# Post-norm transformer layer on one core: a chunk's norm is finished in the third attention step of the next chunk and turned in the fourth, and its first step holds five half groups and nothing else

## The chip, the cores and the metric

The kernel runs on one core of a Trainium2 chip. The metric is device time in microseconds (us), the median of several runs; less is better. The engines are TensorE (matmuls and transposes, PE in the profile; its weight loads are listed as PEld), ScalarE (ACT), VectorE (DVE), GpSimd (POOL) and SyncE (SP), which issues most DMA transfers.

## What is computed

One layer on 2048 tokens of width 256, all float32: attention with 16 heads of 16 channels, a residual add and a layer norm, then a gated feed-forward network with int8 weights and scales, a residual add and a second layer norm.

```python
Q, K, V = X @ Wq + bq, X @ Wk + bk, X @ Wv + bv
scores = einsum('bhqd,bhkd->bhqk', q, k) / sqrt(16)
attn = softmax(scores, axis=-1)
out = einsum('bhqk,bhkd->bhqd', attn, v)          # channels come out as d, h
x = layernorm(X + out @ Wo + bo)
gate, up = silu((x @ w_gate) * s_gate), (x @ w_up) * s_up
x = layernorm(x + ((gate * up) @ w_down) * s_down)
```

## The kernel before

The queries are split into `CH` = 4 chunks of 512 tokens (0 to 3, `LAST` = 3) and the heads into `QUADS` = 4 groups of four. A **step** `s` (0 to 15) is one chunk with one group of heads; steps 4c to 4c+3 are chunk c's attention. A step has 16 **units**, one for each tile of 128 keys (`kt`). A unit's scores for four heads are two **groups** `g` of two heads, each of two banks of PSUM, in a ring of three groups; the matmuls run in fp32r. ScalarE takes the exponential of a group in one instruction (128x1024, line 654). In a **half group** it takes only the second bank; VectorE computes the exponential of the first bank's 512 columns by a polynomial on the bits, eight instructions in a row (lines 884 to 908), the first of which reads PSUM (`bits<-ps`). `poly_tiles(s)` says in which units a step has half groups. TensorE multiplies the probabilities with V two units later (`prob_times_v(u - 2)`, line 1254; `poly` is multiplied in an order in which its tile comes some units later) and sums a whole step in bank 6. At the step's end VectorE copies that bank out (`save_attn`, line 820), which happens while TensorE is in unit 1 of the next step; the next step's first product waits for the copy, and the copy for the last product. Every engine works its own program in order; semaphores tie them, and TensorE's score of group g waits until group g-3 has been read by ScalarE and, if that is a half group, by VectorE.

What is left for chunk c after its attention is spread by hand over the four steps of chunk c+1, which are its **stages** 0 to 3 (`stage = s % QUADS`, with `c = s // QUADS - 1` the finished chunk):

- stage 0: nothing of chunk c but the DMAs that move the results through DRAM into `at32`;
- stage 1: VectorE divides by the denominators (`scale_attn`), TensorE projects quarters 0 and 1 (`project_out`, four matmuls each, line 1276) behind units 8 and 15;
- stage 2: TensorE projects quarters 2 and 3, VectorE adds the first half to x (`ln1_add`, line 836);
- stage 3: the second add, statistics, variance (GpSimd raises it to the power -1/2) and scaling (lines 844 to 864);
- stage 0 of the chunk after: TensorE **turns** the normed tokens, four transposes for each half of the channels (`turn_y`, line 1294), behind units 3 and 8, and VectorE splits each half into a high and a low **part** (`ln1_parts`, lines 871 and 873) that the feed-forward matmuls read.

Chunk 2 has no such stage 0 in the attention: its turn and its parts stand in the feed-forward part, behind chunk 0's gate and up matmuls, where chunk 3's remaining work is spread as well. The attention's small matmuls of all chunks but the last use bank 7 (`FFN_BANK`), one after the other.

In the feed-forward part TensorE computes gate and up (line 1363) tile by tile, then down (line 1340), chunk by chunk. Two of its int8 weights are cast to fp32r by GpSimd (`wg`, `wu`, lines 576 and 577), into the place of the first group's keys, when the last score of step 12 has been computed:

```python
pool.wait_ge(scores_ready, 2 * UPS * (STEPS - QUADS + 1))
nc.gpsimd.tensor_copy(wg[:], gate8[:].bitcast(i8)).then_inc(ffn_w_ready, 1)
nc.gpsimd.tensor_copy(wu[:], up8[:].bitcast(i8)).then_inc(ffn_w_ready, 1)
```

Of the kernel before, what the change touches and what calls it, by code (L numbers as in the profile page):

```python
# [7 lines left out]
def layer_program(nc, X, Wq, bq, Wk, bk, Wv, bv, Wo, bo, w_gate, w_up, w_down, s_gate, s_up, s_down, out):  # L8
# [17 lines left out]
    MT = INTER // P  # L26
    HPB = P // HD
    NQ = 4
    QUADS = NH // NQ
# [26 lines left out]
    with ExitStack() as ctx:  # L56
# [179 lines left out]
        gate_up_free = sem("gate_up_free")  # L236
# [29 lines left out]
        FFN_BANK = 7  # L266


        LAST = CH - 1
# [6 lines left out]

        def turn_bank(c, ko):

            return FFN_BANK if c < LAST - 1 else 2 * ko

        QK = [(c, k) for c in range(CH) for k in (0, 2, 1, 3)]
        NQK = len(QK)
# [23 lines left out]

        def poly_tiles(s):

            return [6, 10, 13] if s == 0 else [2, 6, 10, 13] if s == 1 else [2, 5, 8, 11, 14] if s in (2, 3, 4) else [2, 6, 10, 13]


        def value_order(s):
# [385 lines left out]
        def _(dve):  # L698
# [124 lines left out]
            def scale_attn(c):  # L823

                dve.wait_ge(at_moved, 16 * KO * (c + 1))
                nc.vector.reciprocal(den[:], at32[:, :, HD, :]).then_inc(den_ready, 1)
                dve.wait_ge(den_ready, c + 1)
                nc.vector.tensor_tensor(at32[:, :, 0:HD, :], at32[:, :, 0:HD, :],
                                        den[:].unsqueeze(2).to_broadcast([P, KO, HD, UW]), ALU.mult
                                        ).then_inc(attn_scaled, 1)  # L830

            def ln1_add(c, b):

                bank = out_bank(c, b)
                dve.wait_ge(wo_psum, 2 * c + b + 1)
                nc.vector.tensor_tensor(x_by[:, 2 * b:2 * b + 2, c, :], x_by[:, 2 * b:2 * b + 2, c, :],
                                        ps[:, bank, :].rearrange("p (a b) -> p a b", a=2), ALU.add
                                        ).then_inc(ln1_sum, 1)
# [28 lines left out]
            def ln1_parts(c, ko):  # L867

                bank = turn_bank(c, ko)
                dve.wait_ge(yt_psum, KO * c + ko + 1)  # L870
                nc.vector.tensor_copy(qy[:, c, ko, 0, :], ps[:, bank, :]).then_inc(yt_hi_ready, 1)
                dve.wait_ge(yt_hi_ready, KO * c + ko + 1)
                nc.vector.tensor_tensor(qy[:, c, ko, 1, :], ps[:, bank, :], qy[:, c, ko, 0, :].bitcast(f32), ALU.subtract
                                        ).then_inc(yt_ready, 1)
# [37 lines left out]
            for s in range(STEPS):  # L912
                c = s // QUADS - 1
                if s:
                    save_attn(s - 1)
                tiles = [POLY_NO[2 * (UPS * s + kt)] for kt in poly_tiles(s)]


                stage = s % QUADS
                if s < 2:  # L920
                    for n in tiles:
                        exponentials(n)
                    continue
                exponentials(tiles[0])
                if c >= 0 and stage == 1:
                    scale_attn(c)
                if c >= 0 and stage == 2:
                    ln1_add(c, 0)
                if c >= 0 and stage == 3:
                    ln1_add(c, 1)  # L930
                if c >= 1 and stage == 0:
                    ln1_parts(c - 1, 0)
                exponentials(tiles[1])
                if c >= 0 and stage == 3:
                    ln1_stats(c)
                if c >= 1 and stage == 0:
                    ln1_parts(c - 1, 1)
                exponentials(tiles[2])
                if c >= 0 and stage == 3:
                    ln1_variance(c)  # L940
                for n in tiles[3:]:
                    exponentials(n)
                if c >= 0 and stage == 3:
                    ln1_scale(c)
            save_attn(STEPS - 1)

# [43 lines left out]
            for c in range(CH):  # L990
                for m in range(MT):
                    u = c * MT + m
                    if c and m == 0:
                        scale_down(c - 1)
                    if c == 1 and m == 0:
                        ln1_add(LAST, 0)
                        ln1_add(LAST, 1)
                    dve.wait_ge(silu_done, u + 1)
                    if u >= 2:

                        dve.wait_ge(h_ready, u - 1)
                    nc.vector.scalar_tensor_tensor(h32[:, u % 2, :], ps[:, 2 + u % 2, :], sup_c[:, m:m + 1],  # L1002
                                                   sg[:, u % 2, :], ALU.mult, ALU.mult).then_inc(gate_up_free, 1)
                    if m:
                        h_low(u - 1)
                    if m == MT - 1:
                        h_low(u)

                    if c and m in (2, 3):
                        ln2_stats(c - 1, m - 2)  # L1010
                    if c and m == 4:
                        ln2_variance(c - 1)
                    if c and m in (5, 6):
                        ln2_scale(c - 1, m - 5)


                if c == 0:
                    ln1_parts(LAST - 1, 0)
                    ln1_parts(LAST - 1, 1)
                    scale_attn(LAST)  # L1020
                if c == 1:
                    ln1_stats(LAST)
                    ln1_variance(LAST)
                    ln1_scale(LAST)
                if c == 2:
                    ln1_parts(LAST, 0)
                    ln1_parts(LAST, 1)
# [35 lines left out]
        def _(pe):  # L1063
# [35 lines left out]
            for n, (c, k) in enumerate(QK):  # L1099
# [11 lines left out]
                i, m = k // 2, k % 2  # L1111
# [170 lines left out]
            def turn_y(c, ko):  # L1282

                bank = turn_bank(c, ko)
                if ko == 0 and c >= LAST - 1:

                    pe.wait_ge(gate_up_free, MT - 1 if c < LAST else 3 * MT - 1)
                if ko == 0:
                    pe.wait_ge(ln1_ready, TPC * (c + 1))
                elif c < LAST - 1:  # L1290

                    pe.wait_ge(yt_ready, KO * c + 1)
                for j in range(TPC):
                    last = nc.tensor.transpose(ps[:, bank, j * P:(j + 1) * P], x_by[:, j, c, ko * P:(ko + 1) * P],  # L1294
                                               ident[:])
                last.then_inc(yt_psum, 1)
# [3 lines left out]
            for u in range(UNITS):  # L1300
                scores(2 * u)
                if u == 0:
                    project_v(V_LATE)
                scores(2 * u + 1)
                if u == 1:
                    project_v(V_LATE + 1)
                if u >= 2:
                    prob_times_v(u - 2)
                s, kt = u // UPS, u % UPS
                c, stage = s // QUADS - 1, s % QUADS  # L1310
                if c >= 0 and stage in (1, 2) and kt in (8, 15):
                    project_out(c, 2 * (stage - 1) + kt // 15)
                if c >= 1 and stage == 0 and kt in (3, 8):
                    turn_y(c - 1, kt // 8)
            prob_times_v(UNITS - 2)
            prob_times_v(UNITS - 1)

# [26 lines left out]
            for u in range(CH * MT):  # L1344
                c, m = u // MT, u % MT
                if u == MT:
                    for j in range(TPC):
                        project_out(LAST, j)
                if u == MT + 1:

                    pe.wait_ge(ln1_sum, 2 * CH)
                if m == 0 and c:

                    pe.wait_ge(yt_ready, KO * (CH if c == LAST else LAST))
                if m == 0 and c < LAST:
                    pe.wait_ge(yt_ready, KO * (c + 1))
                if u >= 2:

                    pe.wait_ge(gate_up_free, u - 1)
                for w, bank in ((wg, u % 2), (wu, 2 + u % 2)):  # L1360
                    for ko in range(KO):
                        for part in range(2):
                            last = nc.tensor.matmul(ps[:, bank, :], w[:, ko, m * P:(m + 1) * P], qy[:, c, ko, part, :],  # L1363
                                                    start=(ko == 0 and part == 0), stop=(ko == KO - 1 and part == 1))
                last.then_inc(gate_up_psum, 1)
                if m == MT - 1 and c in (0, LAST - 1):
                    turn_y(LAST if c else LAST - 1, 0)
                    turn_y(LAST if c else LAST - 1, 1)
                if m == MT - 1 and c < LAST:
                    for b in range(c * MT, (c + 1) * MT):  # L1370
                        down(b)
# [38 lines left out]
```

## Time and profile before

| what | value |
|---|---|
| median of 3 runs (lowest to highest) | 600.42 us (600.18 to 600.59) |
| profiled execution, its own time | 600.33 us |
| its span in the profile | 598.6 us |
| TensorE matmuls busy | 588.2 us, 98% |
| ScalarE busy | 506.6 us, 85% |
| VectorE busy | 442.4 us, 74% |
| GpSimd busy | 54.4 us, 9% |
| attention, first save to last | 76.3 to 495.8 us |

Busy time is the time in which at least one instruction of the engine is in flight. Matmuls overlap each other, so a busy TensorE says little about how much more it could do; an engine that waits shows in the waits, not in the busy share. The granted TensorE clock was 0.997 of full speed over the span.

### The profile page before, as it was taken

The numbers are of one execution on the slowest core, as the hardware profiler recorded it, in microseconds if no ns is written. First come the engines' busy times: TensorE is split into PE (matmuls) and PEld (weight loads), VectorE is DVE, ScalarE is ACT, GpSimd is POOL, SyncE is SP. The second block draws the span as 40 slices with busy tenths as digits, with TensorE's granted clock in tenths as the row PEclk, the third lists the DMA queues.
The fourth block names the chain that finished last, engine by engine and source line by source line (L and its number), as shares of the span: only waits on it lengthen the run. The fifth ranks groups of instructions, "written<-read, shape, count | busy, mean of one in ns | idle before, by whom it ended". The sixth has DMA issues, their size and how long they took to land.

```text
span 598.6 us, 10544 instructions
## 1 busy us (share of the span) xinstructions
PE 588.2 (98%) x3952; PEld 249.7 (42%) x3952; DVE 442.4 (74%) x812; ACT 506.6 (85%) x614; POOL 54.4 (9%) x51
## 2 busy tenths in 40 slices
PE   8999999999999999999999999999999999999995
PEld 7884222222222223223232322222323227988974
DVE  6673766989888767687676668888767696776876
ACT  4539999999999999999999999999999995253352
POOL 6606000000000000000000000003000001102021
PEclk9999999999999999999999999999999999999998
DMA  9466938112303020111211010112010000101102
GB/s 207 72 105 85 122 62 105 26 29 35 85 11 70 8 34 8 31 16 25 61 17 27 11 29 11 30 34 44 8 33 7 7 4 9 39 1 35 36 2 71
DMA packets 36185, 24.71 MB, mean 41 GB/s; under 512 B 24930, under 2 KB 30946, under 8 KB 35538
## 3 DMA queue, kind: packets, MB, share of 16 engines
q1 hardware_dynamic: 34740, 23.29, 23.1%
q10 hardware_dynamic: 1392, 0.72, 0.5%
q8 instruction: 32, 0.52, 0.4%
q14 instruction: 21, 0.17, 0.1%
HBM read 6.56 MB, written 4.33 MB: 18 GB/s over the span
## 4 chain that ended last, share of the span: by engine, by line
PE 96%; DVE 2%; ACT 1%; issue 0%; DMA 0%; SPq 0%; POOL 0%; POOLq 0%; ACTq 0%
PE ps L1254 42%; PE ps L1226 29%; PE ps L1363 10%; PE ps L1096 6%; PE ps L1340 4%; PE ps L1276 3%; PE ps L1067 1%; DVE attn_q L820 1%; PE ps L1294 1%; PE ps L1082 1%; ACT probs L654 0%; DMA out<-out_tmp 0%; SPq L511 0%; DVE xt_lo L722 0%; PE ps L1128 0%
## 5 line engine op out<-in xcount | busy, mean ns | idle before, releaser
L654 ACT ACTIVATE probs<-ps 128x1024 f32<-128x1024 f32 (+1 forms) x512 | 444.1, 1098 | 14.8 <-PE ps L1226 14.4
L1254 PE MATMUL ps<-probs,v_all 128*17 128x512 f32 x1916 | 269.0, 598 | 1.2 <-DVE attn_q L820 0.5
L1226 PE MATMUL ps<-q_slot,k_stack 51*128 51x512 f32 x1024 | 198.0, 458 | 0.0
L1226 PEld LDWEIGHTS ps<-q_slot,k_stack 51*128 51x128 f32 x1024 | 85.0, 184 | 220.1 <-ACT probs L654 206.1
L884 DVE TENSOR_SCALAR bits<-ps 128x512 int32<-128x512 f32 x66 | 45.5, 689 | 50.2 <-PE ps L1226 41.3
L1254 PE MATMUL ps<-poly,v_all 128*17 128x512 f32 x132 | 68.2, 599 | 0.0
L673 ACT ACTIVATE sg<-ps,sgate_c 128x512 f32<-128x512 f32 x32 | 22.0, 689 | 49.5 <-PE ps L1363 49.5
L1254 PEld LDWEIGHTS ps<-probs,v_all 128*17 128x17 f32 x1916 | 33.5, 95 | 61.2 <-issue 50.6
L908 DVE SCALAR_TENSOR_TENSOR poly<-poly,bits 128x512 f32<-128x512 f32 x66 | 47.2, 715 | 7.2 <-DVE poly L904 0.5
L904 DVE SCALAR_TENSOR_TENSOR poly<-poly,mant 128x512 f32<-128x512 f32 x66 | 45.7, 692 | 2.3
L895 DVE SCALAR_TENSOR_TENSOR poly<-mant 128x512 f32<-128x512 f32 x66 | 45.2, 684 | 0.0
L900 DVE SCALAR_TENSOR_TENSOR poly<-poly 128x512 f32<-128x512 f32 x66 | 45.1, 684 | 0.0
L820 DVE COPY attn_q<-ps 128x512 f32<-128x512 f32 x16 | 11.1, 691 | 45.3 <-PE ps L1254 45.3
L567 POOL TENSOR_TENSOR rstd<-var_eps,minus_half 128x4 f32<-128x4 f32 x4 | 4.1, 1028 | 402.1 <-DVE var_eps L856 402.1
L1002 DVE SCALAR_TENSOR_TENSOR h<-ps,sup_c,sg 128x512 f32<-128x512 f32 x32 | 23.9, 746 | 16.3 <-ACT sg L673 16.3
L1363 PE MATMUL ps<-qy,wg 128*128 128x512 f32 x128 | 35.6, 400 | 0.0
L1363 PE MATMUL ps<-qy,wu 128*128 128x512 f32 x128 | 34.4, 391 | 0.0
L1340 PE MATMUL ps<-wd,h_hi 128*128 128x256 f32 x128 | 31.1, 285 | 0.0
L1340 PE MATMUL ps<-wd,h_lo 128*128 128x256 f32 x128 | 30.9, 283 | 0.0
L890 DVE TENSOR_SCALAR bits<-bits 128x512 int32<-128x512 int32 x66 | 28.2, 427 | 2.3
L898 DVE TENSOR_SCALAR mant<-mant 128x512 f32<-128x512 f32 x66 | 28.2, 427 | 2.3
L887 DVE TENSOR_SCALAR mant<-bits 128x512 int32<-128x512 int32 x66 | 28.2, 427 | 2.3
(99 smaller groups left out, 452.9 us busy)
## 6 DMA issues: line engine op xcount, KB each, us to landing
q_slot<-qy SPq DMA_DIRECT2D x64, 64.0 KB
k_stack<-k_part SPq DMA_DIRECT2D x12, 256.0 KB
at_dram<-attn_q SPq DMA_DIRECT2D x64, 34.0 KB
at<-at_dram SPq DMA_DIRECT2D x8, 272.0 KB, 3.0
q_slot<-qy SPq DMA_DIRECT2D x64, 32.0 KB
x_tok<-in_L_attn_X SPq DMA_DIRECT2D x14, 128.0 KB, 5.9
k_stack<-k_part SPq DMA_DIRECT2D x12, 128.0 KB
out<-out_tmp SPq DMA_DIRECT2D x12, 128.0 KB, 2.2
```

Source lines behind the costliest of these rows:

```text
L654: nc.scalar.activation(probs[:, slot_of(g), first:2, :].rearrange("p a b -> p (a b)"), ps[:, 2 * ring + first:2 * ring + 2, :].rearrange(" ...
L884: nc.vector.tensor_scalar(bits[:], ps[:, 2 * ring, :], TO_BITS, LOWEST, ALU.mult, ALU.max).then_inc(poly_read, 1)
L887: nc.vector.tensor_scalar(mant[:], bits[:], FRACTION, ONE, ALU.bitwise_and, ALU.bitwise_or).then_inc(poly_bits, 1)
L895: nc.vector.scalar_tensor_tensor(res, mant_f[:], POLY["a"], mant_f[:], ALU.add, ALU.mult).then_inc(poly_square, 1)
L900: nc.vector.scalar_tensor_tensor(res, res, POLY["b"], res, ALU.add, ALU.mult).then_inc(poly_square, 1)
L904: nc.vector.scalar_tensor_tensor(res, res, POLY["c"], mant_f[:], ALU.add, ALU.mult).then_inc(poly_cube, 1)
L908: nc.vector.scalar_tensor_tensor(res, res, POLY["d"], bits_f[:], ALU.add, ALU.mult).then_inc(poly_done, 1)
L1096: last = nc.tensor.matmul(dst, w(ko), x(ko), start=(n == 0), stop=(n == len(terms) - 1))
L1226: last = nc.tensor.matmul(ps[:, 2 * ring + half, :], k_stack[s % QUADS][base:base + ROWS, p, kt * P:(kt + 1) * P], q_slot[slot][base:base ...
L1254: last = nc.tensor.matmul(ps[32 * hh:32 * hh + VW, ACC, :], v_all[:, tiles[hh], NQ * (s % QUADS) + hh, :], prob, start=(kt == 0), stop=(kt ...
L1340: last = nc.tensor.matmul(ps[:, 4 + i, 0:HID], h[:, m, i * P:(i + 1) * P], wd[:, m, :], start=(m == 0 and j == 0), stop=(m == MT - 1 and j ...
L1363: last = nc.tensor.matmul(ps[:, bank, :], w[:, ko, m * P:(m + 1) * P], qy[:, c, ko, part, :], start=(ko == 0 and part == 0), stop=(ko == K ...
```

## The change

The half groups: step 8 and step 12 get five instead of four. The turn of chunks 0 to 2 comes in stage 3, at the same units 3 and 8; chunk 2's leaves the feed-forward part. What made the norm ends in stage 2. For that the projections stand behind units 8 and 13 of stage 1, and 3 and 7 of stage 2. Chunk 3's work stays.

```diff
         def turn_bank(c, ko):
 
-            return FFN_BANK if c < LAST - 1 else 2 * ko
+            return FFN_BANK if c < LAST else 2 * ko
...
-            return [6, 10, 13] if s == 0 else [2, 6, 10, 13] if s == 1 else [2, 5, 8, 11, 14] if s in (2, 3, 4) else [2, 6, 10, 13]
+            return ([6, 10, 13] if s == 0 else [2, 6, 10, 13] if s == 1 or s > QUADS and s % QUADS else
+                    [2, 5, 8, 11, 14])
...
+                if c >= 0 and stage == 2:
+                    ln1_add(c, 0)
                 exponentials(tiles[0])
                 if c >= 0 and stage == 1:
                     scale_attn(c)
+                if c >= 0 and stage == 3:
+                    ln1_parts(c, 0)
+                exponentials(tiles[1])
                 if c >= 0 and stage == 2:
-                    ln1_add(c, 0)
+                    ln1_add(c, 1)
+                    ln1_stats(c)
                 if c >= 0 and stage == 3:
-                    ln1_add(c, 1)
-                if c >= 1 and stage == 0:
-                    ln1_parts(c - 1, 0)
-                exponentials(tiles[1])
-                if c >= 0 and stage == 3:
-                    ln1_stats(c)
-                if c >= 1 and stage == 0:
-                    ln1_parts(c - 1, 1)
+                    ln1_parts(c, 1)
                 exponentials(tiles[2])
-                if c >= 0 and stage == 3:
+                if c >= 0 and stage == 2:
                     ln1_variance(c)
                 for n in tiles[3:]:
                     exponentials(n)
-                if c >= 0 and stage == 3:
+                if c >= 0 and stage == 2:
                     ln1_scale(c)
...
                 if c == 0:
-                    ln1_parts(LAST - 1, 0)
-                    ln1_parts(LAST - 1, 1)
                     scale_attn(LAST)
...
-                if c >= 0 and stage in (1, 2) and kt in (8, 15):
-                    project_out(c, 2 * (stage - 1) + kt // 15)
-                if c >= 1 and stage == 0 and kt in (3, 8):
-                    turn_y(c - 1, kt // 8)
+                if c >= 0 and stage == 1 and kt in (8, 13):
+                    project_out(c, kt // 13)
+                if c >= 0 and stage == 2 and kt in (3, 7):
+                    project_out(c, 2 + kt // 7)
+                if c >= 0 and stage == 3 and kt in (3, 8):
+                    turn_y(c, kt // 8)
...
-                if m == MT - 1 and c in (0, LAST - 1):
-                    turn_y(LAST if c else LAST - 1, 0)
-                    turn_y(LAST if c else LAST - 1, 1)
+                if m == MT - 1 and c == LAST - 1:
+                    turn_y(LAST, 0)
+                    turn_y(LAST, 1)
```

What this does to the order of instructions is best seen at three places. First VectorE at the start of stage 2 of chunk 0 (step 6); before, the rows are the save of step 5, the eight instructions of the first half group's polynomial, and the first add to x:

```order
L820 COPY attn_q_110<-ps 128x512
L884 TENSOR_SCALAR bits<-ps 128x512
L887 TENSOR_SCALAR mant<-bits 128x512
L890 TENSOR_SCALAR bits<-bits 128x512
L895 SCALAR_TENSOR_TENSOR poly<-mant 128x512
L898 TENSOR_SCALAR mant<-mant 128x512
L900 SCALAR_TENSOR_TENSOR poly<-poly 128x512
L904 SCALAR_TENSOR_TENSOR poly<-poly,mant 128x512
L908 SCALAR_TENSOR_TENSOR poly<-poly,bits 128x512
L836 TENSOR_TENSOR x_tok<-x_tok,ps 128x2x256
```

The same place after (line numbers are one higher):

```order
L821 COPY attn_q_110<-ps 128x512
L837 TENSOR_TENSOR x_tok<-x_tok,ps 128x2x256
L885 TENSOR_SCALAR bits<-ps 128x512
L888 TENSOR_SCALAR mant<-bits 128x512
L891 TENSOR_SCALAR bits<-bits 128x512
L896 SCALAR_TENSOR_TENSOR poly<-mant 128x512
L899 TENSOR_SCALAR mant<-mant 128x512
L901 SCALAR_TENSOR_TENSOR poly<-poly 128x512
```

The add has moved ahead of the polynomial, between the save and the reading of the half group's scores.

Second, TensorE in units 13 to 15 of stage 1 and unit 0 of stage 2 (the scores are `q_slot,k_stack`, the products with V `probs,v_all` and `poly,v_all`, a quarter of the projection `wo,at`). Before:

```order
L1226 MATMUL ps<-q_slot_104,k_stack_93 128x512 x4
L1254 MATMUL ps<-probs,v_all 17x512 x4
L1226 MATMUL ps<-q_slot_104,k_stack_93 128x512 x4
L1254 MATMUL ps<-poly,v_all 17x512
L1254 MATMUL ps<-probs,v_all 17x512 x3
L1226 MATMUL ps<-q_slot_104,k_stack_93 128x512 x4
L1254 MATMUL ps<-probs,v_all 17x512 x4
L1276 MATMUL ps<-wo,at_108 128x256 x2
L1226 MATMUL ps<-q_slot_103,k_stack_94 128x512 x4
```

After:

```order
L1224 MATMUL ps<-q_slot_104,k_stack_93 128x512 x4
L1252 MATMUL ps<-probs,v_all 17x512 x4
L1274 MATMUL ps<-wo,at_108 128x256 x2
L1224 MATMUL ps<-q_slot_104,k_stack_93 128x512 x4
L1252 MATMUL ps<-poly,v_all 17x512
L1252 MATMUL ps<-probs,v_all 17x512 x3
L1224 MATMUL ps<-q_slot_104,k_stack_93 128x512 x4
L1252 MATMUL ps<-probs,v_all 17x512 x4
L1224 MATMUL ps<-q_slot_103,k_stack_94 128x512 x4
```

The quarter now stands behind unit 13, which has a half group, instead of behind unit 15.

Third, VectorE in the feed-forward part behind the last h of chunk 0. Before:

```order
L987 TENSOR_TENSOR h_lo<-h_105,h_hi 128x512 x2
L871 CAST qy<-ps 128x512
L873 TENSOR_TENSOR qy<-ps,qy 128x512
L871 CAST qy<-ps 128x512
L873 TENSOR_TENSOR qy<-ps,qy 128x512
L826 RECIPROCAL den<-at_108 128x64
L828 TENSOR_TENSOR at_108<-at_108,den 128x2x512
```

After:

```order
L987 TENSOR_TENSOR h_lo<-h_105,h_hi 128x512 x2
L827 RECIPROCAL den<-at_108 128x64
L829 TENSOR_TENSOR at_108<-at_108,den 128x2x512
L953 TENSOR_TENSOR r_tmp<-ps,sdown_b 128x512 x2
L837 TENSOR_TENSOR x_tok<-x_tok,ps 128x2x256 x2
```

The parts of chunk 2 are gone from there, and the scaling of chunk 3 follows h at once.

## Rows read from the trace of the kernel before

**Rows 1.** Page, part 1: busy us (share of the span) and instructions of each engine.
```profile
PE 588.2 (98%) x3952; PEld 249.7 (42%) x3952; DVE 442.4 (74%) x812; ACT 506.6 (85%) x614; POOL 54.4 (9%) x51
```

**Rows 2.** Waits: engine line waited for, us in total, times, longest us.
```profile
PEld ps L1226 <- ACT probs L654: 206.1, 288, 0.9
```

**Rows 3.** Timeline of TensorE, units 14 and 15 of step 9, unit 0 of 10.
```profile
319.90 0.73 PE L1226 MATMUL ps<-q_slot,k_stack 51*128 51x512 f32 x4
...
321.55 0.73 PE L1226 MATMUL ps<-q_slot,k_stack 51*128 51x512 f32 x4
...
324.26 0.73 PE L1226 MATMUL ps<-q_slot,k_stack 51*128 51x512 f32 x4
```

**Rows 4.** Timelines of ScalarE from four starts (merged rows: start, us, count).
```profile
319.15 5.21 ACT L654 ACTIVATE probs<-ps 128x512 f32<-128x512 f32 x6
...
319.62 4.74 ACT L654 ACTIVATE probs<-ps 128x1024 f32<-128x1024 f32 x5
...
320.53 3.83 ACT L654 ACTIVATE probs<-ps 128x1024 f32<-128x1024 f32 x4
324.80 1.94 ACT L654 ACTIVATE probs<-ps 128x1024 f32<-128x1024 f32 x2 [0.44 <-PE ps L1226]
```

**Rows 5.** Windows, save to save, steps 4 to 8, 15: us, then busy us by engine.
```profile
158.31:185.51 27.20, 27.20 (x194) 7.63 (x194) 23.37 (x41) 27.20 (x34) 0.00 (x0) 1.00 0.31 68
185.51:214.48 28.97, 28.97 (x202) 8.63 (x202) 20.52 (x36) 28.15 (x34) 0.00 (x0) 1.00 0.14 23
214.48:243.28 28.80, 28.67 (x202) 8.52 (x202) 19.41 (x35) 27.97 (x33) 0.00 (x0) 1.00 0.12 19
243.28:270.73 27.45, 27.31 (x194) 7.63 (x194) 22.40 (x47) 27.45 (x33) 1.06 (x1) 1.00 0.13 20
270.73:298.71 27.98, 27.98 (x202) 8.04 (x202) 21.50 (x37) 27.87 (x34) 0.00 (x0) 1.00 0.20 41
...
469.67:495.77 26.10, 25.66 (x185) 6.89 (x186) 22.40 (x47) 26.08 (x30) 1.02 (x1) 1.00 0.05 7
```

**Rows 6.** Timeline at units 2 and 3 of step 10: save, half group, scores.
```profile
327.69 0.69 DVE L820 COPY attn_q<-ps 128x512 f32<-128x512 f32 x1 [4.01 <-PE ps L1254]
328.29 0.68 DVE L884 TENSOR_SCALAR bits<-ps 128x512 int32<-128x512 f32 x1
...
329.41 0.73 PE L1226 MATMUL ps<-q_slot,k_stack 51*128 51x512 f32 x4
```

**Rows 7.** Timelines: end of step 4 (five half groups); end of step 12 with the casts.
```profile
179.13 0.69 DVE L884 TENSOR_SCALAR bits<-ps 128x512 int32<-128x512 f32 x1 [0.27 <-PE ps L1226]
...
180.31 0.73 PE L1226 MATMUL ps<-q_slot,k_stack 51*128 51x512 f32 x4
...
181.38 0.43 DVE L898 TENSOR_SCALAR mant<-mant 128x512 f32<-128x512 f32 x1
...
183.23 0.69 DVE L908 SCALAR_TENSOR_TENSOR poly<-poly,bits 128x512 f32<-128x512 f32 x1
...
184.39 0.61 PE L1254 MATMUL ps<-poly,v_all 128*17 128x512 f32 x1
...
407.22 0.69 DVE L904 SCALAR_TENSOR_TENSOR poly<-poly,mant 128x512 f32<-128x512 f32 x1
407.39 2.27 POOL L576 CAST wg<-gate 128x2048 fp32r<-128x2048 int8 x1 [30.41 <-PE ps L1226]
408.02 2.19 DVE L908 SCALAR_TENSOR_TENSOR poly<-poly,bits 128x512 f32<-128x512 f32 x1
409.62 2.34 POOL L577 CAST wu<-up 128x2048 fp32r<-128x2048 int8 x1
```

**Rows 8.** Chain that ended last, feed-forward part: start us, us, what.
```profile
510.77 0.87 PE ps L1294 x8
...
519.32 3.46 PE ps L1276 x16
```

**Rows 9.** Timeline of VectorE, scaling of chunk 3's results.
```profile
516.80 1.22 DVE L828 TENSOR_TENSOR at<-at,den 128x1024 f32<-128x1024 f32 x1
```

More of the change, by code:

```diff
@@ L1284, in turn_y @@
                 bank = turn_bank(c, ko)
-                if ko == 0 and c >= LAST - 1:
-                    pe.wait_ge(gate_up_free, MT - 1 if c < LAST else 3 * MT - 1)
+                if ko == 0 and c == LAST:
+                    pe.wait_ge(gate_up_free, LAST * MT - 1)
                 if ko == 0:
                     pe.wait_ge(ln1_ready, TPC * (c + 1))
-                elif c < LAST - 1:
+                elif c < LAST:
                     pe.wait_ge(yt_ready, KO * c + 1)
```

## Prediction

> **What bounds the kernel now.** I read the page first, then the waits, then windows from save to save, and last the timeline around the places where the change puts work. The page says TensorE is busy 98% and ScalarE 85% [rows 1]. The waits correct this: TensorE's loads of weights for the scores stood idle 206.1 us for ScalarE's exponentials, in 288 waits [rows 2]. So in the attention the two are nearly matched, and each step must be read for itself.
>
> TensorE needs 321.55 - 319.90 = 1.65 us for a unit (one key tile) when nothing holds it, 26.3 us for a step of 16. A quarter of an output projection put behind a unit adds 324.26 - 321.55 - 1.65 = 1.06 us [rows 3]. ScalarE starts a full exponential every 320.53 - 319.62 = 0.91 us, and a half one lasts 319.62 - 319.15 = 0.47 until the next [rows 4]: 32 x 0.905 - 4 x 0.43 = 27.2 us for a step with four half groups, 26.8 with five.
>
> The windows between saves agree [rows 5]. Plain steps: 27.20 with five half groups (step 4), 27.45 with four (step 7), ScalarE's limit. Steps 5 and 6 with two projections each: 28.97 and 28.80, TensorE's limit of 26.3 + 2 x 1.06 = 28.4 and some edges. Step 8 with two turns and four half groups: 27.98. Steps 9 to 14 repeat 5 to 8, 5 and 6 within 0.02; step 15 is 26.10, since no scores follow it. Behind the attention the chain is TensorE's alone [rows 8].
>
> **The change, part by part**, on the profiled execution's own 600.33 us (span 598.6 and 1.7 around it); the median of the runs shown is 600.42.
>
> (a) Steps 8 and 12 lose both turns and get a fifth half group, so they become like step 4: 27.98 - 27.20 = 0.78, twice, **-1.56**.
>
> (b) Steps 7, 11 and 15 get two turns at units 3 and 8, among the tiles (2, 6, 10, 13) that step 8 has now: 27.98 - 27.45 = 0.53, three times, **+1.59**. Step 15's turn, of chunk 2, is new in the attention.
>
> (c) The feed-forward part loses that turn: 0.87 us of the chain [rows 8], and the down products behind it need only h that is long there. Next would be the projection of chunk 3, which waits for VectorE's scaling of `at32`. It began at 519.32; scaling ended at 516.80 + 1.22 = 518.0, behind 2.8 us of parts that go away [rows 8, 9]. That covers it; without the cover the gain would go. Bounds 0 and 0.87, taken near the row: **-0.83**.
>
> (d) In stage 1 the second projection moves from unit 15 to 13, in stage 2 from 8 and 15 to 3 and 7. TensorE's work stays, and there TensorE is the limit. Only ScalarE's lag behind it grows. A waiting ScalarE starts 324.80 - 324.26 = 0.54 after a unit's first score. At unit 15 it lost 324.80 - (320.53 + 4 x 0.905) = 0.65. With 1.06 put in behind unit 13, where a half group has just used up the slack, the score of unit 14 moves from 319.90 to 320.96, its exponential from 320.53 to 321.50: 0.97 lost [rows 3, 4]. Units 3 and 7 also stand behind half groups. If all of that is paid, it is 0.3 in stage 1 and as much in stage 2; if TensorE's time alone counts, 0. I take +0.27 a chunk, near the middle, as TensorE is the limit in both steps but not in stage 3, where the lag is carried: **+0.8**, between 0 and 1.9.
>
> (e) VectorE's adds, statistics and scaling come one stage earlier. Stage 2 will hold what stage 3 holds now and one add of 0.7 more, 23.1 us of 28.8 [rows 5], and is covered. One place is tight: the first add now stands between the save and the half group of unit 2, so that group's reading of PSUM starts 328.29 - 327.69 = 0.60 later and ends at 329.57. The second score pair of unit 3 writes the same bank, 0.34 behind the first at 329.41, its weights 0.2 before that [rows 6]: late by 0.0 to 0.1, three times. I count 0.1, inside (d)'s figure. If the cover went, it would be 0.6 each.
>
> (f) The fifth half group of step 12. GpSimd casts the two FFN weights right behind the last score of step 12: 407.39 for 2.27 us, 409.62 for 2.34. VectorE's last multiply of tile 13's polynomial started at 408.02 and took 2.19 us, against 0.69 elsewhere: it ended at 410.21, 0.55 behind the first cast's end at 409.66. And the casts' own ends are 1.75 behind VectorE's releases: 407.22 + 0.69 = 407.91 to 409.66, 410.21 to 411.96 [rows 7]. The two engines exclude each other here, instruction by instruction. Today that falls on one multiply and nobody waits. The fifth half group's last tile is 14, a unit later. Take step 4, which has it: the read starts 179.13, the last score ends 180.31 + 0.73 = 181.04, the polynomial ends 183.23 + 0.69 = 183.92, and TensorE wants it at 184.39 [rows 7]. The slack is 0.47. The casts would start at 181.09 on that scale, with the last four operations (2.5 us, 181.38 to 183.92) still to come, the last three of them with two inputs in SBUF like the multiply that was held. The first cast holds them 1.7 us. The second starts with the first's end, finds a chain of separate operations and gets in between them, 1.75 more. The polynomial ends at 183.92 + 1.7 + 1.75 = 187.4, and TensorE's product comes 3.0 late. Behind it stand the save of step 12, the first products of step 13 and its fourth unit, and ScalarE is out of scores by then: nothing covers it. With one cast alone it is 1.7 - 0.47 = 1.2. Bounds: 0, if VectorE's operations slip through, and 3.0. By the row nearest (2.19 for 0.69, handed over at the cast's end) both casts count: **+2.9**.
>
> [...] If only what the row shows is held, two-input operations, the chain stops at 181.72 and not at 181.38, the product is 2.6 late, and the sum is 602.9.
>
> **Sum:** -1.56 + 1.59 - 0.83 + 0.8 + 2.9 = +2.9. 600.33 + 2.9 = 603.2; the median lies 0.1 above the profiled execution at most, so **603.2**.
>
> **Rivals.**
> - *The casts hold only one operation, or none*, because VectorE, once let in at 409.7, keeps the port to the end of its chain. One cast: 0.0 + 1.2, 601.5. None: 600.3. For it: today the waiting multiply did get in ahead of the second cast. Against it: three or four operations are left, not one, and the second cast starts right at the first's end. Chance 0.14 for one, 0.08 for none.
> - *ScalarE is the limit everywhere*, so each gap on it is lost for good. (d) is then its upper end, 1.9, and the sum 604.3. For it: it is busy 27.20 of 27.20 us in step 4; against it, 28.15 of 28.97 and 27.97 of 28.80 in steps 5 and 6, with TensorE at work throughout [rows 5]. It decides if the two projection steps grow together by over 0.4. Chance 0.10.
> - *The change pays, faster.* The turns of stage 3 cost nothing, because ScalarE enters the stage with scores in hand, and the chain of step 12 ends in time: -1.56 - 0.83 = -2.4, 597.9. It needs the polynomial to be done within 0.47 us of slack; from there on it decides. For it: in plain steps TensorE has 27.45 - 26.3 = 1.1 us over. Against it: step 8's 0.53 for the same turns, and (f). Chance 0.05.
> - *The sum as it stands*, both casts, (d) within its bounds: 0.63. Its own range is 602.2 to 604.2.
>
> **How the numbers follow.** The time is the last case's. The range leaves out the case of no cast and the fast one (0.13) and the far end of the ScalarE case: 600.9 to 604.6. About 0.2%, 1.2 us, is what a measurement of this kernel tells from no change: faster than 599.2 is the fast case, 0.06 with an edge; up to 601.6 the none case and most of the one-cast case, 0.18; the rest, 0.76, slower.
>
> **What the profile after would show.** Right: a last multiply (or an operation or two before it) of step 12's fifth polynomial that is stretched to about 2 us, TensorE waiting about 3 us for `poly` in unit 1 of step 13, and the save of step 12 about 3 later than now; step 8 at 27.2; steps 7 and 11 near 28; 0.8 less between the last save and chunk 3's projection. ScalarE's gaps largest behind unit 13 of stage 1 and units 3 and 7 of stage 2. Wrong: that save within 0.5 of where it is (then (f) fails), steps 9 and 10 together over 0.4 longer ((d) or (e) too low), a wait of TensorE for VectorE's add in bank 7, or a wait of chunk 3's projection for `at32`.

## The result and the profile after

The changed kernel takes **606.05 us** (median of 4 runs, 604.72 to 606.22), the kernel before 600.50 in the same job: a ratio of 1.0089, 95% interval 1.0076 to 1.0102. I forecast 603.2, between 600.9 and 604.6. The direction was right; the size was not, and the time lies outside the range. The profiled execution took 605.95 us with a span of 604.2, 5.6 more than before.

Part 1 of the page and the first wait of TensorE's loads hardly moved [rows 1, 2], but for VectorE's 11.3 us more (two more half groups and the time in which it is held), so the averages do not show where the 5.6 us are:

```profile
PE 591.5 (98%) x3952; PEld 250.7 (41%) x3952; DVE 453.7 (75%) x828; ACT 505.5 (84%) x614; POOL 53.9 (9%) x51
```

```profile
PEld ps L1224 <- ACT probs L655: 203.4, 292, 1.7
```

The windows from save to save come next, as in [rows 5], for steps 5 to 8, 12, 13 and 15.

```profile
core 0: us, PE busy (x) PEld busy (x) DVE busy (x) ACT busy (x) POOL busy (x), PEclk, DMA share, GB/s
184.98:214.06 29.08, 29.08 (x202) 8.73 (x202) 20.52 (x35) 27.89 (x33) 0.00 (x0) 1.00 0.13 21
214.06:243.20 29.14, 29.14 (x202) 8.81 (x202) 23.00 (x49) 27.84 (x34) 1.06 (x1) 1.00 0.12 19
243.20:271.18 27.98, 27.98 (x202) 8.03 (x202) 21.50 (x37) 27.86 (x34) 0.00 (x0) 1.00 0.14 22
271.18:298.38 27.20, 27.20 (x194) 7.65 (x194) 23.38 (x41) 27.20 (x34) 0.00 (x0) 1.00 0.20 42
384.55:415.54 30.99, 28.11 (x194) 7.68 (x194) 26.65 (x42) 28.34 (x34) 4.02 (x2) 0.95 0.21 43
415.54:445.97 30.43, 30.43 (x202) 8.88 (x202) 20.62 (x35) 26.95 (x31) 0.00 (x0) 0.93 0.10 15
475.08:501.71 26.63, 26.41 (x193) 7.29 (x194) 21.50 (x37) 26.50 (x31) 0.00 (x0) 1.00 0.05 7
```

Steps 5 to 8 are 29.08, 29.14, 27.98 and 27.20 long, against 28.97, 28.80, 27.45 and 27.98. So what is left of chunk 0 costs 0.20 more than before. Chunk 1 repeats it but for the last of its four steps: step 12 is 30.99 long where step 8 is 27.20, and step 13 is 30.43 where step 9 is 29.06. Of the windows shown, these two alone have a granted clock below 1.00.

The timeline at the end of step 12 shows GpSimd's casts and VectorE's fifth polynomial, as in [rows 7]; the number behind the start is the duration.

```profile
406.89 0.68 DVE L896 SCALAR_TENSOR_TENSOR poly<-mant 128x512 f32<-128x512 f32 x1
407.34 1.98 POOL L577 CAST wg<-gate 128x2048 fp32r<-128x2048 int8 x1 [57.47 <-PE ps L1224]
407.61 2.00 DVE L899 TENSOR_SCALAR mant<-mant 128x512 f32<-128x512 f32 x1
409.28 2.08 POOL L578 CAST wu<-up 128x2048 fp32r<-128x2048 int8 x1
409.53 2.38 DVE L901 SCALAR_TENSOR_TENSOR poly<-poly 128x512 f32<-128x512 f32 x1
411.94 0.69 DVE L905 SCALAR_TENSOR_TENSOR poly<-poly,mant 128x512 f32<-128x512 f32 x1
412.74 0.69 DVE L909 SCALAR_TENSOR_TENSOR poly<-poly,bits 128x512 f32<-128x512 f32 x1
```

Two operations are held, each until a cast ends: line 899, 0.43 us elsewhere, takes 2.00 and ends 0.29 behind the first cast; line 901, 0.69 elsewhere, takes 2.38 and ends 0.55 behind the second. The polynomial ends at 413.43. The same place on TensorE:

```profile
409.82 0.87 PE L1224 MATMUL ps<-q_slot,k_stack 51*128 51x512 f32 x4
413.57 1.01 PE L1252 MATMUL ps<-poly,v_all 128*17 128x512 f32 x1 [2.88 <-DVE poly L909]
415.41 1.22 PE L1224 MATMUL ps<-q_slot,k_stack 51*128 51x512 f32 x4
416.56 1.91 PE L1252 MATMUL ps<-probs,v_all 128*17 128x512 f32 x8
418.40 1.22 PE L1224 MATMUL ps<-q_slot,k_stack 51*128 51x512 f32 x4
419.55 1.05 PE L1252 MATMUL ps<-probs,v_all 128*17 128x512 f32 x8
```

TensorE waits 2.88 us for the polynomial. When it starts again, eight products take 1.91 us, and only from 419.55 on again 1.05. Windows around the place show the granted clock (first number behind the engines' columns):

```profile
407.50:410.50 3.00, 3.00 (x24) 0.87 (x16) 2.96 (x3) 3.00 (x4) 3.00 (x2) 1.00 0.33 54
410.70:412.70 2.00, 0.00 (x0) 0.00 (x0) 1.90 (x2) 2.00 (x3) 0.66 (x1) 1.00 0.44 75
412.72:419.55 6.83, 5.98 (x25) 1.34 (x25) 4.51 (x8) 2.00 (x4) 0.00 (x0) 0.50 0.09 16
419.60:424.00 4.40, 4.40 (x36) 1.12 (x36) 3.07 (x5) 4.40 (x6) 0.00 (x0) 1.00 0.11 15
```

TensorE idles from 410.69 on. At 412.72, still idle, its granted clock falls to 0.50, 1.2 GHz in place of 2.4, and it stays there for 6.83 us. ScalarE is busy 2.00 of these 6.83 us; the rest of the time it waits for scores. The windows of before stand at 1.00 [rows 5]. The Trainium skill ("TensorE: Matmul & The Clock Gate", Part 1: The HAM clock gate) says that an idle TensorE is throttled to 1.2 GHz and that renewed activity releases the throttle. The rows agree: 0.50 came in the idle stretch, and 1.00 came back at 419.55, with TensorE at work again since 413.57. I had not weighed it.

### The profile page after: what moved, and what is told of

The parts are those of the page before. It is cut to its first block, busy times and chain, and to the rows that moved or that the text cites. A ratio compares the mean times of both kernels' runs of the same rounds, so it can differ in the third digit from the quotient of the medians.

```text
span 604.2 us, 10569 instructions
## 1 busy us (share of the span) xinstructions
PE 591.5 (98%) x3952; PEld 250.7 (41%) x3952; DVE 453.7 (75%) x828; ACT 505.5 (84%) x614; POOL 53.9 (9%) x51
## 4 chain that ended last, share of the span: by engine, by line
PE 96%; DVE 2%; ACT 0%; issue 0%; DMA 0%; SPq 0%; POOL 0%; POOLq 0%; DVEq 0%; ACTq 0%
PE ps L1252 41%; PE ps L1224 30%; PE ps L1363 10%; PE ps L1094 6%; PE ps L1340 4%; PE ps L1274 3%; PE ps L1065 1%; PE ps L1292 1%; PE ps L1080 1%; DVE poly L901 0%; DVE mant L899 0%; DMA out<-out_tmp 0%; SPq L512 0%; DVE xt_lo L723 0%; ACT probs L655 0%
## 5 line engine op out<-in xcount | busy, mean ns | idle before, releaser
L885 DVE TENSOR_SCALAR bits<-ps 128x512 int32<-128x512 f32 x68 | 46.9, 690 | 46.2 <-PE ps L1224 37.6
L1252 PE MATMUL ps<-poly,v_all 128*17 128x512 f32 x136 | 71.1, 605 | 2.9 <-DVE poly L909 2.9
L905 DVE SCALAR_TENSOR_TENSOR poly<-poly,mant 128x512 f32<-128x512 f32 x68 | 47.1, 692 | 2.4
L901 DVE SCALAR_TENSOR_TENSOR poly<-poly 128x512 f32<-128x512 f32 x68 | 48.2, 709 | 0.0
L896 DVE SCALAR_TENSOR_TENSOR poly<-mant 128x512 f32<-128x512 f32 x68 | 46.6, 685 | 0.0
L899 DVE TENSOR_SCALAR mant<-mant 128x512 f32<-128x512 f32 x68 | 30.6, 450 | 2.4
```

What stands on the lines that cost most here:

```text
L885: nc.vector.tensor_scalar(bits[:], ps[:, 2 * ring, :], TO_BITS, LOWEST, ALU.mult, ALU.max).then_inc(poly_read, 1)
L896: nc.vector.scalar_tensor_tensor(res, mant_f[:], POLY["a"], mant_f[:], ALU.add, ALU.mult).then_inc(poly_square, 1)
L899: nc.vector.tensor_scalar(mant_f[:], mant_f[:], POLY["e"], POLY["scale"], ALU.add, ALU.mult).then_inc(poly_line, 1)
L901: nc.vector.scalar_tensor_tensor(res, res, POLY["b"], res, ALU.add, ALU.mult).then_inc(poly_square, 1)
L905: nc.vector.scalar_tensor_tensor(res, res, POLY["c"], mant_f[:], ALU.add, ALU.mult).then_inc(poly_cube, 1)
L1252: last = nc.tensor.matmul(ps[32 * hh:32 * hh + VW, ACC, :], v_all[:, tiles[hh], NQ * (s % QUADS) + hh, :], prob, start=(kt == 0), stop=(kt ...
```

## The experiments

Each ran on one chip beside the kernel before, which had a median of 600.54 (first four kernels), 600.36 (next four) and 600.14 us (last four). "Attention" below is the time from the first save to the last in the trace: 419.48 before, 425.96 with the change.

### What step 12 costs

**Four half groups in step 12.**

```
-[2, 6, 10, 13] if s == 1 or s > QUADS and s % QUADS else
+[2, 6, 10, 13] if s in (1, 12) or s > QUADS and s % QUADS else
```

> The changed kernel with step 12 back at four half groups (tiles 2, 6, 10, 13); all else as changed. Theory A (the casts hold the fifth polynomial, TensorE idles 2.9 us, its granted clock falls to 0.5 for 6.8 us and that costs 2.3 more): steps 12 and 13 lose the 5.2 us that they are too long, step 12 is 0.25 longer as a plain step with four half groups, so 606.05 - 5.15 + 0.25 = 601.2, and no stretch of 0.5 clock before the end. Rival B (only the stall of 2.9 comes from the casts, the rest of the miss lies in the moved projections and turns): 606.05 - 2.9 + 0.25 = 603.4.

Measured: 601.35 us, ratio 1.0016 (1.0006 to 1.0025), as theory A had it. Step 12 is 27.62 and step 13 29.09 long, and the granted clock is 1.00 until TensorE's last product is done. Rival B falls.

**Both casts later.**

```
+pool.wait_ge(poly_done, POLY_NO[2 * (UPS * 13 + 6)] + 1)
 nc.gpsimd.tensor_copy(wg[:], gate8[:].bitcast(i8)).then_inc(ffn_w_ready, 1)
+pool.wait_ge(poly_done, POLY_NO[2 * (UPS * 13 + 13)] + 1)
 nc.gpsimd.tensor_copy(wu[:], up8[:].bitcast(i8)).then_inc(ffn_w_ready, 1)
```

> The changed kernel with GpSimd's two casts of FFN weights put where VectorE is idle in step 13: the first behind the polynomial of tile 6 (idle 2.8 us there), the second behind that of tile 13 (idle 4.1 us). Theory A: the fifth half group of step 12 is then free, steps 12 and 13 are as 8 and 9, 606.05 - 5.15 = 600.9. Rival B: 603.2. Rival C (the fifth half group makes step 12 late by itself, since VectorE ends too late there whatever GpSimd does): step 12's stall stays, 606.

Measured: 600.17 us, ratio 0.9993 (0.9984 to 1.0002), 0.7 better than theory A said; behind the last product it has 0.8 less than the changed kernel (see the last section). Windows of steps 12 and 13:

```profile
384.77:411.97 27.20, 27.20 (x194) 7.63 (x194) 23.38 (x41) 27.20 (x34) 0.00 (x0) 1.00 0.21 43
411.97:441.04 29.07, 29.07 (x202) 8.73 (x202) 20.52 (x36) 27.88 (x33) 3.78 (x2) 1.00 0.13 21
```

Both casts now run in step 13, 1.89 us each, and nobody waits. Step 12 with five half groups is as long as step 8. The attention is 420.83, so the collision is worth 425.96 - 420.83 = 5.13 us, all of it in steps 12 and 13. Rivals B and C fall.

**One cast later.** The first added wait of the last edit is left out, the second stays.

> The changed kernel with only the second cast moved behind tile 13 of step 13; the first stays behind the last score of step 12. Theory A: the first cast holds one operation of the polynomial by 1.6 us, of which the slack covers 0.5: TensorE idles 1.2 us, and against the 600.2 of the kernel with both casts moved that gives 601.4 if so short an idle time leaves the granted clock at 1.0, or 603.7 if the clock falls here too. Rival C (one cast is enough for the whole stall): 606.

Measured: 601.71 us, ratio 1.0025 (1.0015 to 1.0035). The rows of VectorE, GpSimd and TensorE at the end of step 12:

```profile
407.83 1.98 POOL L577 CAST wg<-gate 128x2048 fp32r<-128x2048 int8 x1 [57.45 <-PE ps L1225]
408.10 1.99 DVE L900 TENSOR_SCALAR mant<-mant 128x512 f32<-128x512 f32 x1
410.01 0.68 DVE L902 SCALAR_TENSOR_TENSOR poly<-poly 128x512 f32<-128x512 f32 x1
412.36 0.59 PE L1253 MATMUL ps<-poly,v_all 128*17 128x512 f32 x1 [1.18 <-DVE poly L910]
```

One operation is held, TensorE waits 1.18 us (1.2 expected), and the granted clock stays at 1.00; the products behind take 0.6 as ever. The attention is 421.89, 1.06 above that of both casts moved. Rival C falls: the stall of 2.88 needs both casts.

**Work in the wait.** TensorE, in place of idling, transposes the identity 24 times into a bank that nobody reads.

```
+if u == UPS * 13 - 1:
+    pe.wait_ge(yt_ready, KO * 2)
+    for i in range(24):
+        nc.tensor.transpose(ps[:, FFN_BANK, 0:P], ident[:], ident[:])
 if pairs[0] in POLY_NO:
     pe.wait_ge(poly_done, POLY_NO[pairs[0]] + 1)
```

> The changed kernel with 24 transposes of the identity into bank 7, which nobody reads, put before TensorE's wait for the polynomial of tile 14 of step 12: 24 x 0.11 = 2.6 us of work that lies in the idle 2.88 us. Theory A: the polynomial comes as late as before, the save of step 12 stays at 415.5, but the granted clock stays at 1.0 and step 13 is about 2.3 us shorter: 606.05 - 2.3 = 603.7. Rival D (the clock falls for another reason, or its fall costs nothing since ScalarE is the limit): 606.0.

Measured: 603.70 us, ratio 1.0049 (1.0034 to 1.0065). TensorE's rows at the place:

```profile
411.15 2.84 PE L1246 MATMUL ps<-ident 128*128 128x128 f32 x24
414.02 0.60 PE L1256 MATMUL ps<-poly,v_all 128*17 128x512 f32 x1
415.88 1.05 PE L1256 MATMUL ps<-probs,v_all 128*17 128x512 f32 x8
```

The product comes as late as in the changed kernel (414.02 against 413.57, in a run whose first save came 0.53 later); the transposes end as the polynomial does (413.99 and 413.96), so they add next to nothing to the wait. The granted clock stays at 1.00, and the eight products further on take 1.05 and not 1.91. The attention is 423.51. So the 5.13 us split: 423.51 - 420.83 = 2.68 for the wait, 425.96 - 423.51 = **2.45 for the clock**. Rival D falls.

**The kernel before with a fifth half group in step 12**, its turns kept there: `[2, 5, 8, 11, 14] if s in (2, 3, 4, 12) else`.

> The kernel before with a fifth half group in step 12 alone (tiles 2, 5, 8, 11, 14), its turns kept there. Theory A: ScalarE has 0.4 less to do, but the casts hold the last polynomial and the clock falls: 600.4 - 0.4 + 2.9 + 2.3 = 605.2, or more, since VectorE has the parts of the turn in that step too. Rival B: 602.9, with the clock whole. Rival C (the collision needs the rest of the change): 600.0.

Measured: 608.84 us, ratio 1.0139 (1.0123 to 1.0154), 3.6 above theory A's figure; rivals B and C fall. The collision and the clock are there: TensorE waits 3.30 us for the polynomial, and its clock is at 0.5 from 414.58 for 6.83 us. Part of the rest is what theory A named only as "or more". (The profiled execution took 607.19, 1.65 below the median, so the trace does not show all of it.) The waits from 380 to 412 us have a line that the kernel before lacks:

```profile
PE ps L1226 <- DVE bits L884: 1.8, 1, 1.8
```

TensorE's scores wait 1.8 us because VectorE, with five polynomials and two turns' parts in one step (busy 29.13 us, its held time included), reads a score bank late. So the collision needs only the fifth half group, not the rest of the change. The other wait is absent where the turns are out of the step, as in the run with both casts moved.

### What the moved projections cost

**Stage 1's second projection back behind unit 15**, both casts moved: `kt in (8, 15)` in place of `(8, 13)`.

> Both casts moved, and stage 1's second projection back behind unit 15 (stage 2 keeps units 3 and 7). Placement costs ScalarE's lag: the gap behind unit 13 is 0.97 and behind unit 15 it was 0.65, so 0.3 a chunk, 600.2 - 0.9 = 599.3. Rival: TensorE is the limit in that step and the place of its work costs nothing, 600.2.

Measured: 599.83 us, ratio 0.9991 (0.9982 to 1.0000); the attention is 420.48, 0.35 shorter. I expected 0.9, the rival nothing; less than half of the 0.9 came. ScalarE's gap (from one exponential's start to the next, less the 0.91 of a full one) behind the projection did fall from 0.97 to 0.64, but that behind unit 3 of stage 2, now nearer, rose from 0.89 to 0.94 with 0.14 more at unit 2.

**Stage 2 at units 5 and 8**, the rest as in the last: `kt in (5, 8)` in place of `(3, 7)`.

> Both casts moved, stage 1's projections behind units 8 and 15 as before the change, and stage 2's behind 5 and 8 in place of 3 and 7. If it is the half group just ahead (units 2 and 6) that makes the places 3 and 7 dear, stages 1 and 2 come down from 58.12 towards the 57.7 of before: 599.8 - 3 x 0.3 = 598.9. If it is that the projections stand close together, or VectorE's statistics in stage 2: 599.8.

Measured: 599.35 us, ratio 0.9989 (0.9980 to 0.9998), the only version whose interval lies below 1, by a hair. Windows of steps 9 to 12:

```profile
298.51:327.47 28.96, 28.96 (x202) 8.63 (x202) 20.53 (x36) 28.16 (x34) 0.00 (x0) 1.00 0.14 22
327.47:356.47 29.00, 28.85 (x202) 8.60 (x202) 23.10 (x49) 27.81 (x33) 1.02 (x1) 1.00 0.12 19
356.47:384.45 27.98, 27.98 (x202) 8.05 (x202) 21.51 (x38) 27.86 (x34) 0.00 (x0) 1.00 0.11 17
384.45:411.65 27.20, 27.20 (x194) 7.64 (x194) 23.39 (x42) 27.20 (x34) 0.00 (x0) 1.00 0.22 45
```

Step 9 is back at the 28.98 of before, as it was in the last run already; step 10 is 0.2 longer than before. The attention is 420.09, another 0.39 shorter than in the last run, where I expected 0.9; 599.35 lies half-way between the two theories, so the run decides for neither. ScalarE's gaps in step 10 say where the rest sits: 0.64 and 0.73 behind units 5 and 8, against 0.62 and 0.67 behind 8 and 15 before the change, and 0.25 more behind unit 6, the half group that follows the first of them. Why that half group loses 0.25 is left open: the short distance of the two places and VectorE's work there were not told apart.

**Smaller pieces**, with both casts moved and in the kernel before: each projection as two stretches, each turn as two times two transposes. The added lines of the first of the two kernels, without those that let `project_out` and `turn_y` do half of their work; the kernel before has its own places:

```
+PIECES = {1: (8, 10, 12, 14), 2: (3, 5, 7, 8), 3: (3, 4, 7, 8)}
+if c >= 0 and stage and kt in PIECES[stage]:
+    i = PIECES[stage].index(kt)
+    if stage < 3:
+        project_out(c, 2 * (stage - 1) + i // 2, (i % 2,))
+    else:
+        turn_y(c, i // 2, (2 * (i % 2), 2 * (i % 2) + 1))
```

> Both casts moved, and TensorE's additions in pieces of half the size: each projection of 1.06 us as two of 0.53 (behind units 8, 10, 12, 14 of stage 1 and 3, 5, 7, 8 of stage 2), each turn as two times two transposes (behind units 3, 4, 7, 8 of stage 3). Theory: an added stretch costs ScalarE only what goes beyond TensorE's lead of about 0.4 us, so smaller stretches lose less, down to TensorE's own 28.5 us in stages 1 and 2: some 0.9 less for those two stages and 0.4 for stage 3, three chunks, 600.2 - 3.9 = 596.3. Rival (the lead does not grow back between the pieces, each is paid in full): 600.2 or a little more.

> The kernel before, its order of the norm and its four half groups in steps 8 and 12 kept, with the same smaller pieces: projections behind units 8, 10, 12, 15 of stage 1 and 7, 9, 12, 15 of stage 2, turns behind 3, 4, 7, 8 of stage 0. Theory of the lead: 0.6 less in stages 1 and 2 together, three times, and 0.4 in steps 8 and 12, 600.5 - 2.6 = 597.9. Rival (paid in full): 600.5.

Measured: 602.79 us (ratio 1.0038, 1.0024 to 1.0052) and 603.01 us (1.0045, 1.0031 to 1.0059), both slower by 2.6 where I expected 3.9 and 2.6 less. TensorE's timeline, first of the kernel with pieces, then of the one with both casts moved, shows the error:

```profile
311.51 0.70 PE L1276 MATMUL ps<-wo,at 128*128 128x256 f32 x2
312.14 0.73 PE L1226 MATMUL ps<-q_slot,k_stack 51*128 51x512 f32 x4
```

```profile
310.49 1.13 PE L1276 MATMUL ps<-wo,at 128*128 128x256 f32 x4
311.56 0.74 PE L1226 MATMUL ps<-q_slot,k_stack 51*128 51x512 f32 x4
```

From its start to the next score, half a projection takes 0.63 us and a whole one 1.07. So a place costs 0.2 beside its 0.43 for each half, and two places more in a step cost 0.3 to 0.4: step 9 is 29.37 long in place of 29.07. The rival (each piece is paid in full) is nearer but gave 600.2 and 600.5, since it had no cost of a place. The theory that only what goes beyond TensorE's lead is paid was the wrong account.

**Both projections of a stage at one place**, the opposite: behind units 9 and 7, behind 15 and 7, and in the kernel before behind unit 12. Stage 1 of the first kernel:

```
-if c >= 0 and stage == 1 and kt in (8, 13):
-    project_out(c, kt // 13)
+if c >= 0 and stage == 1 and kt == 9:
+    project_out(c, 0)
+    project_out(c, 1)
...
```

> Both casts moved, and both projections of a stage at one place: behind unit 9 of stage 1 and unit 7 of stage 2. The run with halved pieces showed 0.63 us from a half piece's start to the next score and 1.07 for a whole one, so each place costs TensorE 0.19 beside its work. Theory (TensorE's time is what counts in stages 1 and 2): two places fewer in a chunk, 600.2 - 3 x 0.38 = 599.0. Rival (ScalarE's lag counts: a stretch of 1.9 us goes 1.5 beyond the lead of 0.4, as much as two of 1.06 together, or more behind a half group): 600.2 or above.

> As the last, with stage 1's two projections behind unit 15 in place of 9; eight units lie between the two places, and 24 behind the second. Theory of TensorE's time: 599.0 as well. If the spacing matters (TensorE's lead fills up in 24 units and then it waits): 0.2 to 0.4 a chunk more than with 9 and 7.

> The kernel before with both projections of stages 1 and 2 at one place, behind unit 12. Theory of the fixed cost of a place: 0.19 less in each of six steps, 600.4 - 1.1 = 599.3. Rival (ScalarE's lag behind a stretch of 1.9 us): 600.4 or above.

Measured: 600.61 us (ratio 1.0007, 0.9998 to 1.0016), 600.10 us (0.9998, 0.9989 to 1.0007) and 603.04 us (1.0050, 1.0037 to 1.0064). TensorE does save the 0.2, a stretch of eight matmuls takes 1.92 us to the next score. But with 9 and 7 ScalarE's gap behind it is 1.56 to 1.72 us, against 0.71 and 0.97 or 0.89 and 0.82 of two single ones, and the steps are no shorter: 29.15 and 29.15 in place of 29.07 and 29.12. So the theory of TensorE's time (599.0, 599.0 and 599.3) fails, and the rival fits, by which ScalarE's lag behind the longer stretch takes back what TensorE saves (600.2 or above, 600.4 in the kernel before). The run with 15 and 7 was also to tell whether the spacing matters, by 0.2 to 0.4 more a chunk than 9 and 7; it took 0.5 less in all, so that was wrong too. In the kernel before, 1.57 stands against 0.72 + 0.65, with 0.25 more behind unit 13, the half group next to it, as behind unit 6 in the run with 5 and 8. Steps 9 and 10 are 29.21 and 29.20 in place of 28.98 and 28.79, step 11 is 27.63 in place of 27.45. None of the smaller or larger pieces beat single projections; the nearest, 15 and 7, equals the run with both casts moved.

## Why the prediction was wrong

What was added up, and what the traces gave:

| term | predicted | measured | from |
|---|---|---|---|
| (a) steps 8 and 12, without the collision | -1.56 | -1.56 | 27.98 to 27.20, in step 12 with both casts moved |
| (b) steps 7, 11, 15 | +1.59 | +1.60 | 0.53, 0.54, 0.53 |
| (c) turn out of the feed-forward part | -0.83 | -0.71 | last save to last product, 95.59 to 94.88 |
| (d), (e) places of the projections | +0.8 | +1.3 | steps 5 and 6: +0.45; 9 and 10: +0.41; 13 and 14, casts moved: +0.43 |
| (f) the casts and step 12's fifth half group | +2.9 | +5.1 | attention, 425.96 - 420.83 |

These make +5.75. Two things are in no term: the first save comes 0.54 earlier, and 0.35 more lie behind the last product. 5.75 - 0.54 + 0.35 = 5.56, and the span grew by 5.58.

**The failed step is (f), in its size.** Its mechanism came out as written, down to the place: both casts get in, two operations are held, TensorE waits 2.88 us (I said 3.0), and step 12's save comes at 415.54, against 411.97 with both casts moved. The wait by itself costs 2.68. But I wrote "nothing covers it" and then counted the wait's own length as its whole price. After 2.88 us of idle time TensorE came back at half its clock, and in steps where it is nearly the limit that is a second term, 2.45 us. So the upper bound of 3.0 was none: it had to hold a stretch at 0.5 clock as well. The trace of before has such a stretch, 5.91 us from 594.73 on, behind TensorE's last product, and the granted clock is a column of each window in [rows 5].

**Which operations a cast holds.** (f) counts the one-input multiply as held too (603.2); had only two-input operations been held, it would have been 602.9. Line 899 has one input, started at 407.61, 0.27 behind the cast, and took 2.00 us. So the row agrees with the Trainium skill ("SBUF — State Buffer", Who interferes with whom): a VectorE operation in a two-port mode, which a one-input multiply can enter, contends with GpSimd for a shared pair of ports, and the one that issues first has it for its whole instruction while the other waits. The rival "one operation" would have been right with one cast: 1.2 forecast, TensorE's wait 1.18, the attention 1.06 longer.

**(d) was too low.** I took +0.27 a chunk between 0 and 0.6, "as TensorE is the limit in both steps"; it was 0.43. The sign that I had named for this, steps 9 and 10 together over 0.4 longer, is there, if barely (0.41). ScalarE's lag behind unit 13 is the 0.97 that I worked out, but I counted less than half of such lags as lost. The runs that move single places say that ScalarE's lag is the better account: taking unit 13 back to 15 gives 0.35, units 3 and 7 to 5 and 8 gives 0.39, and merging two projections, which saves TensorE's time, gives nothing. It is not the whole account, since I had expected 0.9 of each of the first two. The rival "ScalarE is the limit everywhere" was to be decided by the same 0.4, so its mechanism has more for it than the chance of 0.10 that I gave it; its price, 1.9, is as far above the measured 1.3 as my 0.8 is below.

**(c)** held: from the last save to the last product it is 0.71 less in the changed kernel and 0.82 less (94.77) with both casts moved. Chunk 3's projection does not wait for VectorE's scaling, as I had expected: in the chain, as in [rows 8], the turn's 0.87 is gone and the projection follows the down products at once.

```profile
516.81 7.67 PE ps L1340 x64
524.49 3.46 PE ps L1274 x16
```

**(e)** held: no wait of TensorE for the half group at unit 2 of stage 2 shows in the trace.

**Two slips in the arithmetic of the prediction** change no term. Sixteen units of 1.65 us are 26.4 us and not 26.3. And the windows do not quite agree with ScalarE's computed steps: 27.20 with five half groups where 26.8 was computed, 27.45 with four where it was 27.2. (a) and (b) go by the windows.

Without (f) the change is no gain: +0.2 for each of two chunks, +1.0 for the third, -0.8 in the feed-forward part. The kernel with both casts moved cannot be told from the kernel before (0.9984 to 1.0002).

## What to carry over

A wait of TensorE can have two prices: its length, and the half clock behind it. Here the first cost 2.7 us and the second 2.45, while a wait of 1.18 us had only the first. If a wait cannot be avoided, other work of TensorE put into it can be tried: here it kept the clock at 1.00. Look what GpSimd does in the background before VectorE's work is moved later: a weight cast that can run at any time should wait for a stretch in which VectorE is idle. And where two engines are nearly matched, price an added stretch by the gap that it leaves on the other engine, and count a fixed cost for each place as well as its work.

## What was not expected of the hardware

- The granted clock was at 0.5 for 6.83 us in both kernels where it fell in the attention, behind 2.88 us of idle TensorE in one and 3.30 in the other; the fall came before TensorE started again, at 412.72 and 414.58. The same late product with TensorE kept busy left it at 1.00, as did the 1.18 us of the kernel with one cast.
- The end of the program depends on something other than the kernel's work. From TensorE's last product to the span's end it is 7.6 us in the changed kernel, 7.2 in the one before, and 6.8 with both casts moved, with VectorE's last operations at the same distances in all. The DMA queues of the last 5.6 us of the changed kernel have a line

```profile
q14 instruction: 1, 0.01, 0.3%
```

which is missing in the last 5.6 us of the kernel with both casts moved and of the five others with both moved, all at 6.8 to 6.9; the kernels at 7.2 to 7.6 all have it. So 0.4 to 0.8 us go together with one packet on the instruction queue. That the packet is the cause was not tried, and the six kernels without it are just those with both casts moved, so the runs do not tell the two apart. The shorter end would account for the 0.7 us by which the kernel with both casts moved is better than forecast.
